# State space of a perceiver layer: other units for the B, C and time products, for softplus, and for the z and output products

## What is computed

```python
def _mamba(Z, in_proj_w, conv_w, conv_b, x_proj_w, dt_proj_w, dt_proj_b, A_log, D, out_proj_w):
    xz = jnp.einsum('bld,ed->ble', Z, in_proj_w)
    x, z = jnp.split(xz, 2, axis=-1)
    x = jax.nn.silu(_causal_dw_conv(x, conv_w, conv_b))
    x_dbl = jnp.einsum('bld,ed->ble', x, x_proj_w)
    dt, Bm, Cm = jnp.split(x_dbl, [DTR, DTR + DS], axis=-1)
    dt = jax.nn.softplus(jnp.einsum('blr,dr->bld', dt, dt_proj_w) + dt_proj_b)
    A = -jnp.exp(A_log)
    # h[t] = exp(dt A) h[t-1] + dt B x ;  y[t] = C h[t], 16 states for each of 1024 channels
    y = ys.transpose(1, 0, 2) + x * D
    y = y * jax.nn.silu(z)
    return jnp.einsum('bld,ed->ble', y, out_proj_w)
```

## Time and profile before

| | |
|---|---|
| median of three runs | 4093.0 us |
| the profiled execution | 4091.41 us |
| its span in the profile | 4089.6 us |
| state space: first scan to last scan start | 2495.4 to 3526.9 us |
| steps and units | 8 steps of 32 units, 256 scans |
| mean granted TensorE clock over the span | 0.984 |

### The profile page before, as it was taken

One profiled execution on the slowest core, in us unless ns is written; L12 is line 12 of the kernel. 1 busy time (PEld: TensorE's weight loads), 2 busy tenths in 40 slices (PEclk: granted clock), 3 DMA queues, 4 the chain that ended last, 5 costly groups with the idle time before them and its releaser, 6 DMA issues. The chain is left out here.

```text
span 4089.6 us, 83418 instructions
## 1 busy us (share of the span) xinstructions
PE 3861.8 (94%) x34816; PEld 2797.5 (68%) x34816; DVE 2863.6 (70%) x3017; ACT 1739.5 (43%) x3466; POOL 1153.3 (28%) x547
## 2 busy tenths in 40 slices
PE   8999999999999999999999978999999998699998
PEld 6777877777777787777777755454545553387876
DVE  5667657667666766666776656999999999754433
ACT  2324424423432441442343236776777767322221
POOL 1111111011111111101111104777787678410000
PEclk9999999999999999999999988999999999899999
DMA  4110110010111011101011021210222111220000
GB/s 152 38 42 28 38 52 31 28 50 30 39 39 42 28 38 51 32 28 50 30 38 40 29 99 57 52 53 21 62 57 57 29 44 47 71 77 27 31 21 16
DMA packets 96789, 183.73 MB, mean 45 GB/s; under 512 B 8337, under 2 KB 12817, under 8 KB 96434
## 3 DMA queue, kind: packets, MB, share of 16 engines
q1 hardware_dynamic: 96434, 178.27, 13.9%
HBM read 152.82 MB, written 25.43 MB: 44 GB/s over the span
## 5 line engine op out<-in xcount | busy, mean ns | idle before, releaser
L238 POOL TENSOR_TENSOR c_lo<-c_raw,c_hi 128x2048 fp32r<-128x2048 f32 x64 | 294.5, 4601 | 1972.8 <-DVE c_hi L341 1972.8
L954 POOL TENSOR_TENSOR b_drive<-b_dt_u,b_bc 128x1024 f32<-128x1024 f32 x256 | 600.6, 2359 | 253.0 <-PE b_y L1382 211.9
L429 DVE TENSOR_TENSOR prob_sums<-prob_sums,probs 128x1024 f32<-128x1024 f32 x480 | 566.6, 1222 | 114.0 <-ACT probs L313 114.0
L402 DVE TENSOR_REDUCE max_parts<-scores 128x2 f32<-128x1024 f32 x512 | 601.5, 1217 | 40.2 <-PE scores L563 40.2
L313 ACT ACTIVATE probs<-scores 128x512 f32<-128x512 f32 x1024 | 529.0, 604 | 213.9 <-PE scores L594 213.9
L1236 DVE TENSOR_TENSOR_SCAN b_decay<-b_decay,b_drive 128x1024 f32<-128x1024 f32 x256 | 585.5, 2287 | 19.7 <-ACT b_decay L1103 18.5
L1382 PE MATMUL b_y<-b_drive,b_ident 128*128 128x512 f32 x1024 | 502.4, 619 | 94.6 <-DVE b_drive L1247 94.4
L394 DVE SCALAR_TENSOR_TENSOR k_lo<-scores,bk_sb,k_hi 128x512 fp32r<-128x512 f32 x256 | 192.2, 751 | 564.4 <-ACT k_hi L298 564.4
L298 ACT ACTIVATE k_hi<-scores,bk_sb 128x512 fp32r<-128x512 f32 x256 | 176.3, 689 | 603.7 <-PE scores L515 603.7
L1103 ACT ACTIVATE b_decay<-b_dt,b_a 128x254 f32<-128x254 f32 x1024 | 425.0, 461 | 0.4
L306 ACT COPY v_sb<-scores 128x512 f32<-128x512 f32 x240 | 140.8, 587 | 668.0 <-PE scores L515 668.0
(11 more groups left out here) (220 smaller groups left out, 6278.5 us busy)
## 6 DMA issues: line engine op xcount, KB each, us to landing
c_raw<-in_ctx SPq DMA_DIRECT2D x64, 1024.0 KB, 5.1
b_bc<-bc_scratch SPq DMA_DIRECT2D x128, 256.0 KB, 4.4
q_scratch<-v_sb SPq DMA_DIRECT2D x4, 1024.0 KB, 4.3
q_raw<-q_scratch SPq DMA_DIRECT2D x16, 256.0 KB, 5.1
q_raw<-in_x SPq DMA_DIRECT2D x16, 256.0 KB, 2.9
x_scratch<-q_raw SPq DMA_DIRECT2D x16, 256.0 KB, 5.7
attn_scratch<-attn_out_sb SPq DMA_DIRECT2D x16, 256.0 KB, 2.0
b_attn<-attn_scratch SPq DMA_DIRECT2D x8, 512.0 KB, 4.1
```

The lines of the kernel that those rows point to most:

```text
L238: pool.tensor_tensor(c_lo[:, slot], c_raw[:], c_hi[:, slot].bitcast(F32), ALU.subtract).then_inc(c_lo_ready, 1)
L402: dve.tensor_reduce(max_parts[:, g, 2 * pair:2 * pair + 2, s], max_banks[:, 2 * pair:2 * pair + 2, :], AX.X, ALU.max).then_inc(max_taken, 1)
L429: dve.tensor_tensor(part, part, probs[:, u % 4], ALU.add).then_inc(summed, 1)
L954: pool.tensor_tensor(drive[:, m % 4], dt_u[:, 2 * p:2 * p + 2, :].unsqueeze(1).to_broadcast([P, SG, 2, T]), bc[:, g, 0].unsqueeze(2).to_br ...
```

## The change

It changes numbers in the table that hangs jobs onto units, and nothing else. Every instruction is still there.

```diff
-    PE_HEADS, PE_OUT_LAST, PE_TURN, PE_IN_X, PE_X, PE_DT = (0, 2), 3, 6, (8, 9, 10, 12), 18, (20, 22)
-    PE_IN_Z, PE_OUT = (13, 14, 15, 16, 23, 24, 26, 28), (27, 29, 31)
+    PE_HEADS, PE_OUT_LAST, PE_TURN, PE_IN_X, PE_X, PE_DT = (0, 2), 3, 6, (8, 9, 10, 12), 16, (18, 20)
+    PE_IN_Z, PE_OUT = (13, 14, 15, 17, 22, 23, 25, 26), (27, 28, 30)
     POOL_DT_U1, POOL_DT_H1, POOL_DT_U2, POOL_DT_U3, POOL_RSTD, POOL_OUT = 0, 3, 6, 8, 5, 11
-    POOL_LOW = (27, 31)
+    POOL_LOW = (25, 31)
     POOL_DT_H0 = 30
     ACT_LOG1, ACT_SQUARES, ACT_XN, ACT_XN_T, ACT_SCALE, ACT_TAP, ACT_U = 1, 8, 7, 9, 13, (11, 12, 14, 16), 17
-    ACT_Z, ACT_DBC, ACT_ABS, ACT_EXP = (18, 19, 26, 31), 21, (23, 25), (24, 26)
-    ACT_ROUND, ACT_LOG0, ACT_GATE = (24, 27), 28, 4
+    ACT_Z, ACT_DBC, ACT_ABS, ACT_EXP = (18, 20, 26, 29), 19, (21, 24), (22, 25)
+    ACT_ROUND, ACT_LOG0, ACT_GATE = (22, 29), 27, 4
```

## The result

| | before | after |
|---|---|---|
| median of 20 runs each | 4092.3 us | 4101.3 us |
| lowest and highest | 4088.1 to 4093.9 | 4097.9 to 4104.3 |
| profiled execution, span | 4089.6 us | 4099.5 us |
| first scan to last scan start | 1031.49 us | 1038.95 us |

The ratio is 1.0023, with a 95% interval of 1.0016 to 1.0029: 9.0 us slower, between 6.5 and 11.9. Of the 9.9 us between the two spans, 7.46 lie between the first and the last scan. Another 0.65 were there before the first scan and 0.85 came in the feed-forward part, neither of which the change touches; over the kernels of this study the first scan started anywhere from 2493.7 to 2497.9. The remaining 0.93 is the end of the last step.

What follows compares the result with a forecast made beforehand. VectorE's chain of scan and product was taken to set the state space's pace. +0.6 us a step over seven steps (+4.2) plus +0.6 at the end gave +4.8 on 4093.0: 4097.8 us, range 4090 to 4106.

Steps and rivals of the forecast that it cites:

- B, C and time product hidden, operand there in time: TensorE, units 16 to 18: VectorE hides these jobs; operand u is ready three us before TensorE asks.
- rival C: Moved B, C product stalls TensorE waiting for silu, delaying jobs up to sum 31; 4104.8 us, chance 0.07.
- Softplus, first half, +0.5: Scan of unit 23 comes late because ScalarE waits for the time product: +0.5 us a step, bounds 0 to 1.0.
- Logarithm, 1.76 goes and 0.3 comes: ScalarE's logarithm moves from unit 28 to 27: unit 29's 1.76 us wait goes, 0.3 comes at unit 28.
- Output products, +2.8: Third output product ahead of sum 31 makes end_pair of the next unit 0 wait: +2.8 us a step.
- Unit 2, -0.75: VectorE reaches add_heads in unit 2 after TensorE's heads product is done: 0.75 us gained a step.
- no cost, but no room: GpSimd's drive for unit 0 again ends 0.3 us ahead of the scan, so the change costs nothing there.
- Sum per step: All terms of one step: +0.8 us added up, +0.6 by clock times (the walk); +0.6 taken, ends -0.2 and +1.5.
- Seven steps: +4.2: State space: the +0.6 us a step applied to seven steps, +4.2 us.
- Last step's end, +0.6: End of last step: end_pair comes 3.4 us later, but only end_pair itself is newly exposed, +0.6 us.
- Rival A: TensorE at half clock around unit 6 makes unit 8's end_pair wait: total +7.6, worse form +12.6 us; chance 0.20.
- Rival B: TensorE's sum 31 is in time for unit 0, leaving only ScalarE's terms: 4084.8 us, chance 0.07.

Runs made afterwards that it cites:

- e3: On top of e1_out31, the z half of unit 17 moved to unit 19 behind the first time product, its take_z to unit 23: 4080.9 us, ratio 0.9976.
- e5_before_log_first: Kernel before, with only the logarithm in unit 27, second rounding in 29 and first-half rounding error in 25: 4091.8 us against 4090.9, ratio 1.0002.
- The first two experiments: e1_out31 and e2_before_out30, which put the third output product behind or ahead of sum 31: 4087.7 us and 4115.3 us.
- e6: On top of e4, logarithm moved to unit 25, second-half exponential to 27, first-half rounding error to 24: 4071.0 us, ratio 0.9951.
- e1_out31: The change, with the third output product put back from unit 30 to unit 31, behind sum 31: 4087.7 us against 4091.4 before, ratio 0.9990.
- e2_before_out30: Kernel before, with only its third output product moved from unit 31 to unit 30: 4115.3 us, ratio 1.0060.
- e4: On top of e3, VectorE takes the first half of the heads product in unit 3 instead of 2: 4070.1 us, ratio 0.9949; again 4069.9 us.
- e8: On top of e6, GpSimd's make_dt of the first half in unit 29 instead of 30: 4066.6 us against 4091.0 before, ratio 0.9937.

## Why the prediction came out as it did

The median of 4101.3 lies in the range of 4090 to 4106, 3.5 us above the 4097.8 forecast. The change itself was +9.0 where the sum was +4.8, so the way it moved, the places and the causes were right, and the forecast was little more than half of the size. In the profile the state space and the end of the last step make +8.4; the 3.6 above the sum are 1.9 from the sum per step, 1.2 from the seventh step, 0.3 from the end of the last, and 0.2 from unit 8 and rounding. The other 1.5 of the profile's 9.9 lie in the two parts that the change does not touch. The verdict that I called likeliest, within 0.2%, is missed by a hair: the measured change is 0.23%, its interval lies on both sides of the bound, and I had 0.23 on slower.

- **B, C and time product hidden, operand there in time**: right. TensorE did not stop ahead of it, and rival C did not occur.
- **Softplus, first half, +0.5**: right in cause and place. The wait was 0.60 and the step lost 0.68. The third experiment (e3) shows the cause.
- **Unit 24, -0.3**: -0.36.
- **Logarithm, 1.76 goes and 0.3 comes**: -1.83 and +0.38. The load and the logarithm took the same time as before, 2.25 us to the next copy. Of the two reasons, a backlog and the rounding beside it, `e5_before_log_first` leaves 0.3 to the second.
- **Output products, +2.8, "the term that decides"**: the wait was 2.77, the step lost 2.90. TensorE's queue took 19.07 us where I had 19.1. The first two experiments show it from both sides.
- **Unit 2, -0.75**: -0.85 where it exists.
- **GpSimd "no cost, but no room"**: right; e6 ran into it as soon as 0.38 us were taken out elsewhere.
- **Sum per step**: too small. My terms added up to +0.8, the walk by clock times gave +0.6, and I took the walk. It measured +0.92. Against the scan of unit 16, the walk was 0.22 us early at the scan of unit 23 already, and 0.33 at scan 3. The term that was mis-sized is softplus's first half, 0.68 where I had 0.5: TensorE's time product came 0.10 later than in the walk, and the rest lies in the handing over from engine to engine. The other terms are off by 0.10 or less and nearly cancel. Each wait costs 0.07 to 0.13 us more than its idle time in the trace, as the scan or `end_pair` behind a wait loses its overlap with the one ahead (a product's row has 1.22, the next scan starts 1.14 after it). That doesn't explain the miss: for the three new waits it adds 0.29, and for the three that went it gives 0.29 back.
- **"Seven steps: +4.2"**: mis-sized as well. The `end_pair` of unit 0 is waited for seven times, but only six of those steps have an `add_heads` to give 0.75 back. The seventh set of terms, ScalarE's in the first step and `end_pair` in the last, pays +1.8, not +0.6. With +0.92 and this, the state space comes to +7.3.
- **Last step's end, +0.6**: +0.93 in the trace, mis-sized by 0.3. The mechanism holds (`end_pair` waited 5.39 us there instead of 2.08, and the fourth output product took back most of it).
- **Rival A, half clock around unit 6**: the mechanism exists, the link to the change does not show. Leaving out the first step, which paid 0.61 in both, three steps paid 0.6 to 0.7 before (1, 3, 4) and three after (2, 4, 6). My argument for it, the additional idle time of 1.2 us ahead of unit 5, is not borne out: the change has that gap and had three such steps of 1 to 6, `e1_out31` does not have it and had six. Its worse form, half clock from the sum of unit 6 into the sum of unit 7, came at full length once, in step 6 of `e2_before_out30`, where the wait was 2.06 and I had 1.4.
- **Rival B**: out, the queue was as full as its rows said.

## What to carry to other kernels

In an in-order queue the price of a job is paid by whatever stands behind it. Before moving a filler job up, look for the instruction behind it that another engine waits for without slack, here the last sum of a group, and keep long jobs behind that one. When terms of about 1 us cancel, count for each how many iterations really have it, first and last included, and price a wait by the distance between the instructions around it rather than by the idle time alone. And walk all engines: when ScalarE's wait of 0.30 at unit 28 was removed in e6, GpSimd stood 0.32 behind it at unit 0.

## What the runs showed of the hardware

An idle gap of 2.67 us in front of the sum of unit 6 was followed by the half clock (1.2 instead of 2.4 GHz) in some steps and not in others: 1, 3 and 4 before, 2, 4 and 6 after, and all from 1 to 6 in `e1_out31`. Over 8 us from 1 us after the start of unit 6's scan, the granted clock was 0.78 or 0.79 in these steps and 1.00 in the others. With 1.77 us of idling, in e4, e6 and e8, it did not occur in steps 1 to 6, nor with the gap filled. The length of the last gap is not all that counts: in the first step that gap is 2.13 us, and the half clock followed it in the six traces where TensorE had idled 3.0 us one sum earlier, and in none of the four (e4 twice, e6, e8) where it had idled 1.75. The Trainium skill (TensorE: Matmul & The Clock Gate, Part 1) says that the gate's timing runs free of the program; that like steps differ agrees with it, while no run here changed that timing alone.
